# Five full expert tiles taken out of the first choice and computed around the boundary between attention and the experts

## The chip, the cores and the metric

The kernel runs on one core of one Trainium2 chip. The metric is the device time of one execution in microseconds (us); lower is better. The engines are named as in the profile: PE (TensorE), DVE (VectorE), ACT (ScalarE), POOL (GpSimd) and SP (SyncE, which here only issues DMAs). The fp32 operands of the large products are taken as pairs of fp16 numbers, a high part and what is left of it ("hi" and "lo" in many names).

## The reference

```python
def reference(x, ctx_1024, g_xattn, g_ffn, ...):      # x: (4, 2048, 512), context: (4, 77, 512)
    x = x + tanh(g_xattn) * xattn(layernorm(x), ctx_1024)   # layer norm, q, 16 heads of 64, softmax, w_out, gate
    # mixture of experts: 8 true experts and 2 null ones, top 2 of 10
    weights, selected = top_k(softmax(x @ gate_w.T + gate_b), 2)
    true_weights = weights * (selected < 8)
    norm_w = true_weights / (sum(true_weights) or 1)
    out = sum over the chosen true experts e of norm_w * (LN(x) @ expert_w[e] + expert_b[e])
    return x + tanh(g_ffn) * out
```

The text of the last lines is shortened: the experts get layernorm(x) of the new x. There are 8192 tokens, so that every token has two choices, each for a true expert or for none.

## The kernel before, in words

The program has three blocks, and all engines meet at the end of each.

**fold_context** (118 us) turns the context and the attention weights into two small matrices for each batch.

**attend** (L591) goes over the 8192 tokens in 64 tiles of 128. It is a software pipeline: each engine has a function `step` for a turn i (it calls the parts for tile i, i-1, i-2, ...) and a function `tail` for the last turns, i = 64 to 67. The order of the calls in `step` and `tail` is the order on the engine. In turn i, PE multiplies the scores of tile i (L908) and the mix of tile i-2 (L923); DVE does the softmax of tile i-1 (L1133, L1135), the new x of tile i-3 (`residual`, L1152) and its statistics, and after POOL's power (`y_rstd`, L1499) the normalized y (`y_normalize`, L1169); ACT and POOL split y in two fp16 parts (L1042, L1503); SP transposes them by DMA (`turn_y`, L809) and stores x and y to `comb` in HBM (`store`, L828); PE multiplies the gate logits (`gate`, L955, one turn later). The last tile's y is transposed by PE (L939, "turn_last") and its gate comes last. Four tiles are a group. For each group DVE finds the two experts of every token and its place among the tokens of that expert (L1195 to L1330), with running counts in `placed`, and POOL writes the entries (token number, weight, mean, 1/std) into `table` with eight indirect DMAs a group (`scatter`, L1597). The table has a region of 64 tiles for each of 8 experts and each of 2 choices.

At the end PE sums the counts of all 16 groups (`totals`, L1002), DVE rounds them up to tiles (`count_tiles`, L1609 to L1621) and works out which expert and which place in the table each tile of the list has (`find_tiles(0)`, L1627 to L1635). ACT multiplies the experts' bias (L1090), which SP loads with the last DMA of the block (L889).

**run_experts** (L1667) goes over tiles of 128 tokens of one expert, first all tiles of choice 0, then those of choice 1, in passes of five (`RING`); the number of tiles is rounded up to full passes, which gives 50 tiles in choice 0 and 70 in choice 1. For a tile, SP loads its slice of the table (`slots`, L1769, at a place read into a register, L1775), DVE makes the token numbers (L1940), POOL gathers x of 128 tokens (L1799), ACT normalizes it (L1908), PE transposes it (L1862, 4 instructions), ACT and DVE split it (L1900, L1953), PE multiplies (L1875, 12 instructions), DVE adds the bias and x (L1963, L1988), and POOL scatters the result (L1820): back to `comb` in choice 0, to the output in choice 1. PE begins the block with 14 matmuls of no use (`WARM`, L1854) while the first slots and tokens come. POOL has the last scatters of the table between the gathers of tiles 3 and 4, and DVE runs `find_tiles(1)` while it waits for the first tile.

## Time and profile before

| | |
|---|---|
| median of 3 runs | 1365.33 us (1365.13 to 1366.55) |
| the profiled execution | 1363.62 us, span 1361.8 us |
| fold_context | 0 to 118.9 us |
| attend | 118.9 to 959.4 us, PE busy 821 of 840 |
| run_experts | 959.4 to 1361.8 us, PE busy 378 of 402 |
| PE, DVE, ACT, POOL busy | 96%, 81%, 55%, 50% of the span |
| granted TensorE clock, mean | 0.982 |

The span is the time on the engines; the execution's own time is 1.8 us longer. Times in a row count from the span's start. A row of the timeline gives the start, the duration, the engine, the line and what it did; in brackets stands the idle time before it and what released it. "Issue" is time in which the engine waited for nothing that the profile shows.

### The profile page before, as it was taken

To read this page: it belongs to the slowest core of one execution; us is meant where nothing else is said; L and a number is where in the kernel's file an instruction comes from. 1 tells how busy PE (TensorE), PEld (TensorE's weight loads), DVE (VectorE), ACT (ScalarE), POOL (GpSimd) and SP (SyncE) were. 2 spreads that over 40 slices of the span, in tenths; PEclk is the share of its full clock that TensorE was granted. 3 is DMA by queue.
4 is the path that set the end of the run, shared out by engine and by line. 5 is a ranking of instruction groups with operands and counts; after the bars stand their busy time and mean duration, and the time that the engine had idled before them with its cause. 6 is when DMAs were issued, how large, how long until landed. Compare 5 with 4: busy or idle time off the path is not lost. (4 is left out here: it accounts for less than half of the span.)

```text
span 1361.8 us, 30170 instructions
## 1 busy us (share of the span) xinstructions
PE 1302.1 (96%) x7339; PEld 674.7 (50%) x7340; DVE 1109.2 (81%) x2797; ACT 752.8 (55%) x2724; POOL 686.4 (50%) x645
## 2 busy tenths in 40 slices
PE   7999999999999999999999999996699988999997
PEld 5434555555555555555555555553355544555554
DVE  5776888998998998998998999987577765777775
ACT  4755666656656656656656656663444433444442
POOL 1501233446445455455455455445676755776674
PEclk9999999999999999999999999998799998999999
DMA  8144888778978778978778978877355535787773
GB/s 310 54 170 129 184 195 193 182 186 200 243 183 192 181 181 210 239 180 193 180 180 212 238 180 194 181 160 194 80 163 163 160 130 178 234 250 244 242 240 117
DMA packets 413298, 256.17 MB, mean 188 GB/s; under 512 B 338979, under 2 KB 350307, under 8 KB 413077
## 3 DMA queue, kind: packets, MB, share of 16 engines
q1 hardware_dynamic: 385365, 180.89, 54.9%
q0 software_dynamic: 27840, 74.18, 17.3%
q8 instruction: 41, 0.67, 0.2%
q14 instruction: 52, 0.43, 0.1%
HBM read 111.61 MB, written 75.01 MB: 137 GB/s over the span
## 5 line engine op out<-in xcount | busy, mean ns | idle before, releaser
L1023 ACT ACTIVATE expd<-scores,less 128x77 f32<-128x77 f32 x1024 | 317.4, 328 | 183.0 <-DVE less L1127 182.0
L908 PE MATMUL scores<-arena,zT 128*128 (+2 forms) x2304 | 414.8, 339 | 3.4 <-PEq L159 3.4
L923 PE MATMUL mix<-u_sb,pT 128*128 128x512 f16 x1728 | 383.5, 380 | 1.3 <-DMA pT<-p_parts 0.7
L1875 PE MATMUL out_bank<-arena,expert_yT 128*128 x1440 | 336.1, 384 | 0.0
L908 PEld LDWEIGHTS scores<-arena,zT 128*128 128x128 f16 x2304 | 220.7, 98 | 170.0 <-issue 5.8
L923 PEld LDWEIGHTS mix<-u_sb,pT 128*128 128x128 f16 x1728 | 168.8, 98 | 198.5 <-DVE x_out L1152 1.4
L1875 PEld LDWEIGHTS out_bank<-arena,expert_yT 128*128 128x128 f16 x1440 | 142.5, 99 | 148.1 <-issue 7.5
L1023 ACT ACTIVATION_READ_ACCUMULATOR expd<-scores,less 128x1 f32 x1024 | 213.5, 209 | 0.0
L1597 POOL DMA_INDIRECT table<-payload,row_i x128 | 159.7, 1248 | 60.1 <-issue 34.9
L1900 ACT CAST expert_yT<-yT_bank 128x512 f16<-128x512 f32 x120 | 70.2, 585 | 182.6 <-PE yT_bank L1862 180.9
L1494 POOL TENSOR_TENSOR z_parts<-z,z_parts 128x512 f16<-128x512 f32 x62 | 71.7, 1156 | 193.4 <-ACT z_parts L1014 193.4
L1988 DVE SCALAR_TENSOR_TENSOR result<-out_bank,slots,biased 128x512 f32<-128x512 f32 x120 | 90.1, 751 | 70.5 <-PE out_bank L1875 68.1
L1499 POOL TENSOR_TENSOR x_moments<-x_spread,minus_half 128x1 f32<-128x1 f32 x64 | 65.0, 1015 | 131.3 <-DVE x_spread L1162 131.2
L1953 DVE TENSOR_TENSOR expert_yT<-yT_bank,expert_yT 128x512 f16<-128x512 f32 x120 | 83.0, 691 | 46.6 <-ACT expert_yT L1900 45.0
L1125 DVE TENSOR_REDUCE top<-scores 128x5 f32<-128x385 f32 (+1 forms) x192 | 111.4, 580 | 3.5 <-PE scores L908 3.4
L1135 DVE SCALAR_TENSOR_TENSOR expd<-expd,inverse 128x1232 f32<-128x1232 f32 x64 | 92.3, 1442 | 2.2
L1799 POOL DMA_INDIRECT two_ring<-comb,token x66 | 71.1, 1077 | 45.1 <-issue 31.6
L1143 DVE TENSOR_TENSOR p_parts<-expd,p_parts 128x1232 f16<-128x1232 f32 x64 | 91.8, 1435 | 0.2 <-issue 0.2
L1862 PE MATMUL yT_bank<-ident,expert_y 128*128 128x128 f32 x480 | 74.7, 279 | 17.2 <-ACT expert_y L1908 13.7
L1820 POOL DMA_INDIRECT out_dram<-result,token_out x70 | 72.9, 1042 | 28.2 <-issue 19.0
L1862 PEld LDWEIGHTS yT_bank<-ident,expert_y 128*128 128x128 f32 x480 | 59.7, 143 | 44.2 <-ACT expert_y L1908 20.6
L1035 ACT CAST p_parts<-expd 128x1232 f16<-128x1232 f32 x64 | 77.7, 1214 | 0.0
(183 smaller groups left out, 1643.2 us busy)
## 6 DMA issues: line engine op xcount, KB each, us to landing
comb<-x_out SPq DMA_DIRECT2D x64, 512.0 KB, 3.2
x_ln<-in_x_dram SPq DMA_DIRECT2D x64, 256.0 KB
x_res<-in_x_dram SPq DMA_DIRECT2D x64, 256.0 KB, 2.8
w_raw<-in_L_ffn_expert_w_dram SPq DMA_DIRECT2D x64, 128.0 KB, 2.3
u_dram<-u_stage SPq DMA_DIRECT2D x12, 512.0 KB, 2.8
u_sb<-u_dram SPq DMA_DIRECT2D x6, 1024.0 KB, 7.6
arena<-in_L_xattn_w_kv_dram SPq DMA_DIRECT2D x4, 1024.0 KB, 7.5
slots<-table SPq DMA_DIRECT2D x150, 2.0 KB
```

The lines of the kernel that those rows point to most:

```text
L908: last = pe.matmul(scores[s][k][:, 0:n], zT[:, s, zp, t, :], m, start=(t == 0 and (zp, mp) == PRODUCTS[0]), stop=(t == DT - 1 and (zp, mp) ...
L923: last = pe.matmul(mix[:], pT[:, s, pp, k, :], u_sb[:, k, up, :], start=(k == 0 and (pp, up) == PRODUCTS[0]), stop=False)
L1023: last = act.activation(expd[:, s, h * KEYS:(h + 1) * KEYS], scores[s][k][:, at:at + KEYS], ACT.Exp, bias=less[:, s, h:h + 1], scale=1.0 / ...
L1035: act.copy(p_parts[:, 0, 0:COLS], expd[:, s, :]).then_inc(p_hi_ready, 1)
L1125: dve.tensor_reduce(top[:, s, h0:h0 + nh], bank, AX_X, ALU.max).then_inc(top_ready, 1)
L1135: dve.scalar_tensor_tensor(e, e, P_SCALE, inverse[:, s].unsqueeze(2).broadcast_to([P, HEADS, KEYS]), ALU.mult, ALU.mult).then_inc(p_ready, 1)
L1143: dve.tensor_tensor(p_parts[:, 1, 0:COLS], expd[:, s, :], p_parts[:, 0, 0:COLS], ALU.subtract).then_inc(p_lo_ready, 1)
L1597: pool.indirect_dma_start(table, bass.IndirectOffsetOnAxis(ap=self.row_i[:, side, TOP_K * t + k:TOP_K * t + k + 1], axis=0), self.payload[ ...
L1862: last = pe.transpose(c.yT_bank[s][:, t, :], y[:, s, t * P:(t + 1) * P], ident[:])
L1875: last = pe.matmul(c.out_bank[s][:], yT[:, s, yp, t, :], w_of[:, bass.ds(e, 1), t, wp * D:(wp + 1) * D].rearrange("p a n -> p (a n)"), sta ...
L1953: dve.tensor_tensor(yT[:, s, 1], c.yT_bank[s][:], yT[:, s, 0], ALU.subtract).then_inc(c.y_lo_ready, 1)
L1988: dve.scalar_tensor_tensor(result[:, s, :], c.out_bank[buffer(s)][:], own, biased[:, buffer(s), :], ALU.mult, ALU.add).then_inc(c.result_r ...
```

## The change

Five tiles of choice 0 are taken out of the experts' passes. They are tiles that are full after twelve of the sixteen groups; the counts of twelve groups are enough to know five of them.

- PE sums the counts at the end of turn 60, and waits in turn 61, ahead of `gate`, until DVE has read them. DVE finds experts and places of the five tiles in 17 small instructions spread over turn 61 (`head_1` to `head_13`), and what is taken from each expert in 5 more in turn 62 (`take_1` to `take_4`). At the end of turn 62 it waits for the five table slices and makes the token numbers.
- SP loads the five slices in turn 62 (`fetch_head`: a register load and five DMAs behind the second transposition of p).
- POOL gathers three of the tiles at the end of turn 63 and two in the tail of turn 64, ahead of four scatters of the table. `result` is cleared at the start of attend.
- ACT normalizes them and casts the high parts (`split_head`, tails of turns 64 and 65), POOL subtracts the low parts (`low_head`, tails of 65 and 66), SP transposes them (`turn_head`), two ahead of the last `turn_y` and three behind it.
- PE multiplies three of them after `totals`, in attend's block, and two at the start of the experts' block, in place of the 14 matmuls of no use.
- DVE finishes them at the start of the experts' block (`finish_head`, two instructions a tile): two ahead of the first tokens, three behind. POOL scatters one ahead of the first gathers, four between the fourth gather and the last scatters of the table. `find_tiles(1)` moves into the first pass, in two parts, behind tiles 0 and 1. The transposes of tile 1 wait until all five are finished.
- Choice 0 has five tiles fewer in its list: 45 in place of 50. The `PSUM` banks are shared between the blocks, buffers are laid out in another order, and the semaphores of the first block are freed and used again.

```diff
+HEAD_GROUP = GROUPS - 4
+HEAD_BANKS = (3, 1, 2, 4, 5)
+HEAD_SOON = 3
...
+            def fetch_head():
+                sp.wait_ge(listing.head_listed, 1)
+                spots = table.rearrange("(p t) w -> p t w", p=P)
+                places = nc.values_load_multi_w_load_instructions(
+                    listing.head_at[0:1, :], (sp.engine,), min_val=0, max_val=TABLE_TILES - 1,
+                    skip_runtime_bounds_check_because="head_13 clamps it")[1]
+                for j, place in enumerate(places):
+                    sp.dma_start(listing.head_slots[:, j, :],
+                                 spots[:, bass.ds(place, 1), :].rearrange("p a w -> p (a w)")).then_inc(
+                                     listing.head_entry_in, 16)
...
+            def turn_head(j):
+                sp.wait_ge(listing.head_lo_ready, j + 1)
+                sp.dma_start_transpose(out=head_yT[:, j].rearrange("p l t q -> p (l t) q"),
+                                       in_=head_parts(ln, j).rearrange("p l d -> p (l d)")).then_inc(listing.head_yT_in[j], 16)
...
+                if isinstance(i, int) and i == TILES - 2:
+                    fetch_head()
...
+                if i == TILES + 1:
+                    turn_head(0)
+                    turn_head(1)
+                if i == TILES + 2:
+                    turn_head(2)
+                    turn_head(3)
+                    turn_head(4)
...
+                    if isinstance(i, int) and i == TILES - 3:
+                        pe.wait_ge(listing.head_done, 1)
...
+                if isinstance(i, int) and i == TILES - 4:
+                    pe.wait_ge(listing.head_placed_ready, GROUPS - 3)
+                    pe.matmul(totals, ones16[:], listing.head_placed[:], start=True, stop=True).then_inc(
+                        listing.head_counted, 1)
...
+            pe.wait_ge(w_lo_ready, TILES)
+            multiply_head(nc, pe, listing, banks, head_yT, w_parts, range(HEAD_SOON))
...
+            def split_head(j):
+                act.wait_ge(listing.head_got[j], 16)
+                act.activation(head_y[j], listing.result[:, j, :], ACT.Identity, bias=listing.head_slots[:, j, 2:3],
+                               scale=listing.head_slots[:, j, 3:4]).then_inc(listing.head_y_ready, 1)
+                act.wait_ge(listing.head_y_ready, j + 1)
+                act.copy(head_parts(ln, j)[:, 0], head_y[j]).then_inc(listing.head_hi_ready, 1)
...
+                    act.wait_ge(z_lo_ready, TILES)
+                    act.wait_ge(zT_in[0], landed(TILES - 2, 0))
+                    split_head(0)
+                    split_head(1)
+                if i == TILES + 1:
+                    split_head(2)
+                    split_head(3)
+                    split_head(4)
...
+                heads = isinstance(i, int) and i == TILES - 3
+                takes = isinstance(i, int) and i == TILES - 2
...
+                if heads:
+                    listing.head_1(dve, totals)
+                if takes:
+                    listing.take_1(dve)
...
+                    listing.head_13(dve)
+                if takes:
+                    dve.wait_ge(listing.head_entry_in, 16 * RING)
+                    own = listing.head_slots[:, :, 0:1]
+                    dve.tensor_scalar(listing.head_token[:], own, 2.0, None, ALU.mult).then_inc(listing.head_token_ready, 1)
...
+            listing.find_owners(dve, 0)
+            listing.find_places(dve, 0).then_inc(listing.listed, 1)
...
+            def gather_head(j):
+                pool.wait_ge(listing.head_token_ready, 1)
+                pool.wait_ge(listing.result_clear, 1)
+                halves = comb[0:HEAD_GROUP * GROUP * P].rearrange("n (l d) -> (n l) d", l=2)
+                pool.indirect_dma_start(listing.result[:, j, :], None, halves,
+                                        bass.IndirectOffsetOnAxis(ap=listing.head_token[:, j, :], axis=0),
+                                        bounds_check=halves.shape[0] - 1, oob_is_err=False).then_inc(listing.head_got[j], 16)
+            def low_head(j):
+                pool.wait_ge(listing.head_hi_ready, j + 1)
+                parts = head_parts(ln, j)
+                pool.tensor_tensor(parts[:, 1], head_y[j], parts[:, 0], ALU.subtract).then_inc(listing.head_lo_ready, 1)
...
             def tail(i, s, turn):
                 ps, t = 1 - s, (i - 3) % GROUP
                 if live(i - 3):
                     y_rstd(i - 3, ps, t)
                 if i == TILES:
+                    gather_head(3)
+                    gather_head(4)
+                if i == TILES + 2:
+                    low_head(2)
+                    low_head(3)
+                    low_head(4)
+                if i == TILES:
                     scatter(GROUPS - 3, ((1, 1), (2, 0), (2, 1), (3, 0)))
                 if i == TILES + 1:
                     scatter(GROUPS - 3, ((3, 1),))
                     scatter(GROUPS - 2, ((0, 0),), by_choice=True)
+                    low_head(0)
+                    low_head(1)
...
+                if isinstance(i, int) and i == TILES - 1:
+                    gather_head(0)
+                    gather_head(1)
+                    gather_head(2)
...
+            pool.memset(listing.result[:].rearrange("p s d -> p (s d)"), 0.0).then_inc(listing.result_clear, 1)
             run(pool, step, tail)
...
+def multiply_head(nc, pe, listing, banks, head_yT, w_parts, tiles):
+    w_of = w_parts.rearrange("p (e t) x -> p e t x", t=DT)
+    pe.wait_ge(listing.head_listed, 1)
+    chosen = nc.values_load_multi_w_load_instructions(
+        listing.head_expert[0:1, tiles.start:tiles.stop], (pe.engine,), min_val=0, max_val=EXPERTS - 1,
+        skip_runtime_bounds_check_because="head_9 clamps it")[1]
+    for j, e in zip(tiles, chosen):
+        pe.wait_ge(listing.head_yT_in[j], 16)
+        for t in range(DT):
+            for yp, wp in PRODUCTS:
+                last = pe.matmul(banks[HEAD_BANKS[j]][:], head_yT[:, j, yp, t, :],
+                                 w_of[:, bass.ds(e, 1), t, wp * D:(wp + 1) * D].rearrange("p a n -> p (a n)"),
+                                 start=(t == 0 and (yp, wp) == PRODUCTS[0]),
+                                 stop=(t == DT - 1 and (yp, wp) == PRODUCTS[-1]))
+        last.then_inc(listing.head_summed, 1)
...
+        dve.wait_ge(self.taken_ready, 4)
+        self.after(dve, dve.tensor_tensor(self.tiles_f[:], self.tiles_i[:], self.taken[:], ALU.subtract))
+        dve.tensor_tensor(self.held[:], self.tiles_f[:], self.taken_turn[:], ALU.subtract)
...
+            def scatter_head(j):
+                pool.wait_ge(listing.head_result, j + 1)
+                pool.wait_ge(listing.head_token_ready, 2)
+                pool.indirect_dma_start(halves, bass.IndirectOffsetOnAxis(ap=listing.head_token_out[:, j, :], axis=0),
+                                        result[:, j, :], None, bounds_check=halves.shape[0] - 1,
+                                        oob_is_err=False).then_inc(listing.head_put[j], 16)
...
+            scatter_head(0)
             for j in range(LEAD):
                 gathers(choices[0], j, j)
+            for j in range(1, R):
+                scatter_head(j)
...
-            for n in range(WARM):
-                again = pe.matmul(spare_bank[:], w_of[:, 0, n % DT, 0:P], w_of[:, 1, n % DT, 0:D], start=True, stop=True)
-            again.then_inc(warmed, 1)
+            multiply_head(nc, pe, listing, banks, head_yT, w_parts, range(HEAD_SOON, R))
...
+                elif c.k == 0 and j == 1:
+                    pe.wait_ge(listing.head_result, R)
...
+            head_experts = nc.values_load_multi_w_load_instructions(
+                listing.head_expert[0:1, :], (dve.engine,), min_val=0, max_val=EXPERTS - 1,
+                skip_runtime_bounds_check_because="head_9 clamps it")[1]
+            def finish_head(j):
+                own = listing.head_slots[:, j, 1:2]
+                dve.scalar_tensor_tensor(result[:, j, :],
+                                         expert_bias[:, bass.ds(head_experts[j], 1), :].rearrange("p a n -> p (a n)"), own,
+                                         result[:, j, :], ALU.mult, ALU.add).then_inc(listing.head_biased, 1)
+                dve.wait_ge(listing.head_biased, j + 1)
+                dve.wait_ge(listing.head_summed, j + 1)
+                dve.scalar_tensor_tensor(result[:, j, :], banks[HEAD_BANKS[j]][:], own, result[:, j, :], ALU.mult,
+                                         ALU.add).then_inc(listing.head_result, 1)
...
+            finish_head(0)
+            finish_head(1)
             for j in range(R):
                 if j in (0, FIRST):
                     dve.wait_ge(entry_in[j // FIRST], 16 * (FIRST if j == 0 else R - FIRST))
                 name_token(choices[0], 0, j, j)
-            listing.find_tiles(dve, 1).then_inc(listing.listed, 1)
+            for j in range(2, R):
+                finish_head(j)
...
+                    if c.k == 0 and first_pass(r) and s == 0:
+                        listing.find_owners(dve, 1)
+                    if c.k == 0 and first_pass(r) and s == 1:
+                        listing.find_places(dve, 1).then_inc(listing.listed, 1)
```

POOL at the end of attend, before: from `y_low(60)` on (L1597 is `scatter`, L1499 `y_rstd`, L1503 `y_low`).

```order
L1503 TENSOR_TENSOR y_parts<-y,y_parts 128x512
L1597 DMA table<-payload,row_i 135168x4 x3
L1499 TENSOR_TENSOR x_moments<-x_spread,minus_half 128x1
L1597 DMA table<-payload,row_i 135168x4 x4
L1499 TENSOR_TENSOR x_moments<-x_spread,minus_half 128x1
L1597 DMA table<-payload,row_i 135168x4 x2
L1499 TENSOR_TENSOR x_moments<-x_spread,minus_half 128x1
L1597 DMA table<-payload,row_i 135168x4 x9
```

The same stretch of the change, behind `y_low(60)` (L1864 is `scatter`, L1601 `y_rstd`, L1621 `gather_head`, L1628 `low_head`).

```order
L1864 DMA table<-payload,row_i 135168x4 x3
L1621 DMA result<-comb,head_token 128x512 x3
L1601 TENSOR_TENSOR x_moments<-x_spread,minus_half 128x1
L1621 DMA result<-comb,head_token 128x512 x2
L1864 DMA table<-payload,row_i 135168x4 x4
L1601 TENSOR_TENSOR x_moments<-x_spread,minus_half 128x1
L1864 DMA table<-payload,row_i 135168x4 x2
L1628 TENSOR_TENSOR z_parts<-z,z_parts 128x512
L1628 TENSOR_TENSOR arena<-z,arena 128x512
L1601 TENSOR_TENSOR x_moments<-x_spread,minus_half 128x1
L1628 TENSOR_TENSOR arena<-x_ln,arena 128x512 x2
L1628 TENSOR_TENSOR arena<-gamma,arena 128x512
L1864 DMA table<-payload,row_i 135168x4 x9
```

The five gathers stand ahead of `y_rstd` of tiles 61 and 62, and two of the subtractions ahead of that of tile 63.

SP at the end of attend, before, from the last transpositions of p on (L824 `turn_p_lo`, L809 `turn_y`, L828 `store`, L889 the experts' bias).

```order
L824 DMA_TRANSPOSE pT<-p_parts 128x10x128
L809 DMA_TRANSPOSE yT<-y_parts 128x8x128
L778 DMA x_res<-in_x_dram 128x512
L828 DMA comb<-x_out 256x1x512
L809 DMA_TRANSPOSE yT<-y_parts 128x8x128
L828 DMA comb<-x_out 256x1x512
L889 DMA u_sb<-in_L_ffn_expert_b_dram 128x4096
```

The same stretch of the change (L831, L816, L835, L922; L852 is `turn_head`, L785 the load of x).

```order
L831 DMA_TRANSPOSE pT<-p_parts 128x10x128
L816 DMA_TRANSPOSE yT<-y_parts 128x8x128
L785 DMA x_res<-in_x_dram 128x512
L835 DMA comb<-x_out 256x1x512
L852 DMA_TRANSPOSE arena<-z_parts 128x8x128
L852 DMA_TRANSPOSE arena<-arena 128x8x128
L816 DMA_TRANSPOSE yT<-y_parts 128x8x128
L835 DMA comb<-x_out 256x1x512
L852 DMA_TRANSPOSE arena<-arena 128x8x128 x3
L922 DMA u_sb<-in_L_ffn_expert_b_dram 128x4096
```

Two transpositions of the five tiles stand ahead of the last `turn_y`, which is that of tile 62, and three ahead of the load of the bias.

POOL at the start of the experts, of the change (L2097 is `scatter_head`, L2069 the gathers, L1864 the scatters of the table; before, the block began with one scatter of the table, four gathers and five scatters of the table).

```order
L1864 DMA table<-payload,row_i 135168x4
L2097 DMA comb<-result,head_token_out 16384x512
L2069 DMA one_ring<-comb,token 128x512 x4
L2097 DMA comb<-result,head_token_out 16384x512 x4
L1864 DMA table<-payload,row_i 135168x4 x5
```

One scatter of a result has gone ahead of the first gather, and four ahead of the five scatters of the table and the fifth gather.


## Rows read from the trace of the kernel before

**Rows 1.** Timeline of PE, end of attend and start of the experts.

```profile
939.43 0.18 PE L955 MATMUL routing<-gate_parts,yT 128*128 128x20 f16 x1 [0.45 <-DMA yT<-y_parts]
...
942.01 1.12 PE L939 MATMUL scores<-ident,y 128*128 128x128 f32 x4 [2.23 <-DVE y L1169]
...
950.43 0.19 PE L1002 MATMUL routing<-placed,ones 128*128 128x16 f16 x1 [1.91 <-DVE placed L1313]
959.50 4.53 PE L1854 MATMUL spare_bank<-arena 128*128 128x512 f16 x14 [8.88 <-PEq L598]
```

**Rows 2.** Busy time by stretch: length, each engine, PEclk, DMA share, GB/s.

```profile
942.00:962.00 20.00, 4.54 (x24) 2.26 (x25) 11.49 (x66) 6.75 (x4) 10.72 (x10) 0.50 0.31 110
...
970.00:975.00 5.00, 4.81 (x14) 2.28 (x15) 2.00 (x4) 2.38 (x4) 3.78 (x5) 0.50 0.19 52
```

**Rows 3.** Chain that ended last, start of the experts: start, us, what.

```profile
959.46 0.75 SPq L1775
...
961.00 1.67 DMA slots<-table
...
963.76 3.43 DMA one_ring<-comb,token
...
971.31 4.92 PE out_bank L1875 x12
976.23 0.44 PE yT_bank L1862 x4
976.66 2.59 PE out_bank L1875 x12
```

**Rows 4.** Timeline of DVE, turn 62 and the last turns of attend.

```profile
911.58 0.25 DVE L1133 RECIPROCAL inverse<-total 128x16 f32<-128x16 f32 x1 [1.41 <-ACT expd L1023]
...
928.17 0.54 DVE L1169 TENSOR_SCALAR y<-x_out,x_moments 128x512 f32<-128x512 f32 x1
...
931.42 0.69 DVE L1152 SCALAR_TENSOR_TENSOR x_out<-mix,x_res 128x512 f32<-128x512 f32 x1 [0.24 <-PE mix L928]
...
934.13 0.55 DVE L1169 TENSOR_SCALAR y<-x_out,x_moments 128x512 f32<-128x512 f32 x1 [0.47 <-POOL x_moments L1499]
...
938.83 0.69 DVE L1152 SCALAR_TENSOR_TENSOR x_out<-mix,x_res 128x512 f32<-128x512 f32 x1 [0.93 <-PE mix L928]
...
941.41 0.55 DVE L1169 TENSOR_SCALAR y<-x_out,x_moments 128x512 f32<-128x512 f32 x1 [0.69 <-POOL x_moments L1499]
```

**Rows 5.** Timeline of SP (its queue), same stretch and the slots.

```profile
906.90 1.53 SPq L824 DMA_TRANSPOSE pT<-p_parts  x1
...
936.27 1.27 SPq L809 DMA_TRANSPOSE yT<-y_parts  x1
...
960.47 6.12 SPq L1769 DMA_DIRECT2D slots<-table  x10
```

**Rows 6.** Timeline of POOL, same stretch.

```profile
920.58 1.16 POOL L1503 TENSOR_TENSOR y_parts<-y,y_parts 128x512 f16<-128x512 f32 x1 [4.81 <-ACT y_parts L1042]
...
933.40 0.69 POOL L1499 TENSOR_TENSOR x_moments<-x_spread,minus_half 128x1 f32<-128x1 f32 x1
...
938.83 0.98 POOL L1597 DMA_INDIRECT table<-payload,row_i  x1 [3.24 <-DVE payload L1330]
...
944.72 1.05 POOL L1597 DMA_INDIRECT table<-payload,row_i  x1 [3.34 <-issue]
```

**Rows 7.** Timeline of POOL, the fifth gather of the experts.

```profile
975.92 1.04 POOL L1799 DMA_INDIRECT one_ring<-comb,token  x1 [0.30 <-issue]
```

**Rows 8.** Timeline of ACT, end of attend.

```profile
948.55 3.62 ACT L1090 ACTIVATE u_sb<-u_sb 128x4096 f32<-128x4096 f32 x1 [1.42 <-DMA u_sb<-in_L_ffn_expert_b_dram]
```

**Rows 9.** Timeline of DVE, one y in turn 61.

```profile
895.91 1.50 DVE L1169 TENSOR_SCALAR y<-x_out,x_moments 128x512 f32<-128x512 f32 x1
```

**Rows 10.** Chain that ended last, after 45 tiles of the experts.

```profile
1109.40 3.41 issue
...
1113.89 3.64 PE out_bank L1875 x12
```

More of the change, by code:

```diff
@@ new lines, in __init__ @@
+        self.head_got = [sem(f"head_got{s}") for s in range(RING)]
+        self.head_y_ready = sem("head_y_ready")
+        self.head_hi_ready = sem("head_hi_ready")
+        self.head_lo_ready = sem("head_lo_ready")
+        self.head_yT_in = [sem(f"head_yT_in{s}") for s in range(RING)]
+        self.head_summed = sem("head_summed")
+        self.head_biased = sem("head_biased")
+        self.head_result = sem("head_result")
+        self.head_put = [sem(f"head_put{s}") for s in range(RING)]
```

185 lines of the change are left out of this document (159 added, 26 removed).

## The prediction

> **What bounds the kernel now.** I read the page's slices first: PE is busy nine tenths or more of almost every slice. The timeline of PE then shows where it isn't: at the end of attend [rows 1]. From 939.43 to 959.50 PE does under 5 us of work. It waits for DVE's last y (2.23 us idle before 942.01), sums the counts at 950.43 and is idle for 8.88 us until the next block's matmuls of no use. So this stretch is bound by latency: one chain over DVE, POOL, SP and PE, in which each microsecond put into any link is paid in full. The windows show the clock with it [rows 2]: granted 0.50 (1.2 GHz) from 942 to 962 and again from 970 to 975, where the mean of the span is 0.98 of 2.4 GHz. The chain of waits through the start of the experts [rows 3] is a register load (0.75), slots (1.67 to land), a gather (3.43), then tile 0, which multiplies for 4.92 us at the low clock. Later tiles take 2.59 and 0.44 for their transposes, and follow one another: 3.03 each.
>
> **What is saved.** One pass of choice 0 is five tiles: 5 x 3.03 = 15.1 us [rows 3]. That holds only as far as the rest isn't lengthened. The multiplication of the five tiles is not saved but moved to where PE is idle; what the change must win is the idle time at the boundary.
>
> **What is added, link by link.** DVE's 17 small instructions in turn 61 and 5 in turn 62 (about 0.1 us each, an estimate) I cost at nothing: DVE was idle for 1.41 us at the end of a turn, waiting for ACT [rows 4]. If the cover is short, up to 17 x 0.1 is added, in the range.
>
> 1. *The five table slices.* SP issues them behind `turn_p_lo(61)`, which ends at 906.90 + 1.53 = 908.4 [rows 5]. A register load (0.75), five issues at 6.12/10 = 0.61 and 1.67 to land [rows 3, 5] give 913.9. DVE waits for them at the end of turn 62, where it went on at 911.58 [rows 4]. With the token numbers: 914.2, **+2.6**. Everything behind on DVE goes with it, the y that POOL waits for too.
> 2. *Three gathers ahead of `y_rstd(61)`.* POOL's subtraction ended at 920.58 + 1.16 = 921.7 [rows 6]; with 2.6 it is 924.3. Three scatters at 0.98 + 0.30 [rows 6, 7] give 928.3 with their lag, three gathers at 1.04 + 0.30 [rows 7] 932.4, the power (0.6) 933.1: y(61) begins there instead of at 928.17 [rows 4], +5.0. Of that the 0.24 us idle before x_out(62) is taken up: +4.8 there.
> 3. *Two gathers ahead of `y_rstd(62)`.* From 933.1: two gathers 2.7, four scatters 5.1, the power 0.6 [rows 6, 7]: y(62) at 941.7 instead of 934.13 [rows 4], +7.6. In the trace DVE then worked until 938.83 - 0.93, so 3.8 us: x_out(63) at 945.6 instead of 938.83.
> 4. *Two subtractions ahead of `y_rstd(63)`.* The scatter at 938.83 began 0.93 us after DVE's payload [rows 4, 6], so now at 946.5, and takes 0.98. Two subtractions of 1.16 end at 950.0. y(63) follows at about 950.7 instead of 941.41.
> 5. *SP.* `turn_head(1)` waits for the second subtraction and stands ahead of `turn_y(62)`. A transposition holds the queue 1.3 us, so that of y(62) is issued at 951.6. In the trace its gate came 939.43 - 936.27 = 3.2 us behind the issue [rows 1, 5]: 954.8. The transposes of y(63) stand behind that gate on PE: 955.0 instead of 942.01, **+13.0**. This contains links 1 to 4. SP's order costs 3.7 of it, since y(63) alone would have let PE begin at 951.3.
> 6. *From there to the counts* nothing moves: 8.42 us [rows 1], totals at 963.4. The three last `turn_head` and the bias load end on SP at 959; the bias needs 8.4 us to land by the page, and ACT 3.6 for its multiplication [rows 8], which ends at about 971, beside link 7.
> 7. *PE's three tiles.* A register load 0.75 and 36 matmuls. At 2.59/12 they take 7.8; a start at the low clock cost the 14 of `WARM` 4.53 - 3.02 = 1.5 more and tile 0 2.3 more [rows 1, 3]. I take 9.5 in all. So PE ends at 963.6 + 10.3 = 973.9, where DVE and POOL needed 8.88 us behind the counts [rows 1]: PE is last by 1.4. The block's change is about 0.2 to 0.3. The experts begin at 974.1 instead of 959.50: **+14.6**.
> 8. *The start of the experts.* DVE loads five registers and runs four instructions of some 0.8 ahead of the first tokens: 4.0 to 4.2 us against 3.2 until the slots came, **+1.0**. POOL has four scatters of a result (4 x 1.3) ahead of the fifth gather. That gather was issued at 975.92 [rows 7] and lands 3.4 later; PE needed its y at about 982.3, with 0.8 for ACT: a slack of some 2.1 against 5.2 later: **+3.1** before tile 3 or 4. Two tiles in place of `WARM` (24 against 14 matmuls) end while PE waits anyhow.
>
> The Trainium skill, page "DMA: Bandwidth & Descriptors", section "Anatomy of one DMA — SWDGE (gpsimd) path", gives a DMA about 2.0 us and its bytes over 436e3. That would be an estimate of 2.6 us for the 256 KB of a gather; the row has 3.43 [rows 3], and I use the row. By the page the stall before tile 4 would be 0.8 shorter.
>
> Another row speaks against the change. One y took 1.50 us in turn 61 instead of 0.54, as a POOL subtraction ran beside it [rows 4, 9]. The change puts five such subtractions into the tail, where DVE is on the chain; I count none of them as hit, and up to 1 us for each of two in the range. The Trainium skill, page "SBUF — State Buffer", section "SBUF: two separate sides", says why: DVE and GpSimd share one pair of ports, which whoever starts first has until its instruction ends. By that rule alone the sum would be about 1 to 2 us higher.
>
> **The sum.** 14.6 + 1.0 + 3.1 - 15.1 = **+3.6 us**. Against the profiled execution that is 1363.6 + 3.6 = 1367.2. The median of the runs shown lies 1.7 above it, so I forecast 1368.9. A difference of 0.2% (2.7 us) is about what a measurement of this kernel can tell from none: "the same" is 1362.6 to 1368.1.
>
> **Rivals.**
>
> *A, SP's order costs nothing (chance 0.20).* The slices land before DVE asks for them, and y(62) isn't held by the transpositions ahead of it. For: SP had over 2 us between its DMAs there, and the landing may overlap the issues more than I have it. Against: the order on SP is fixed. It decides where y(63) and not gate(62) releases the transposes. It gives back 2.6 and 3.7: 1368.9 - 6.3 = 1362.6, the edge of faster and the same.
>
> *B, the stall behind the 45th tile goes (0.18).* PE was idle there for 3.41 us for no reason that the profile shows, and multiplied the next tile in 3.64 instead of 2.59 [rows 3, 10]; with 0.6 for its transposes at the low clock these are 5.1 us on the way to choice 1. It came at the end of a loop. A program of another layout may not have it: 1363.8.
>
> *C, POOL pauses on the chain (0.13).* Behind the last `y_rstd` POOL did nothing for 3.34 us, for no reason shown, with work in its queue [rows 6]. Then it cost nothing. If it stands ahead of a subtraction or `y_rstd` now, each of the links behind is later by it: 1368.9 + 3.3 = 1372.2.
>
> *D, the list isn't shorter (0.03).* If the counts still fill ten passes, nothing is saved: 1384.
>
> **Numbers.** The forecast has 0.46: 0.04 faster, 0.12 the same (its terms for the start and the clock may be 1 us too high), 0.30 slower. A: 0.14 faster, 0.06 the same. B: 0.07, 0.10, 0.01 slower. C and D are slower. Together 0.25, 0.28 and 0.47. The range goes from 1361.0 (A, with 1.5 less from the start) to 1374.0 (C, with two blocked DVE instructions); it leaves out D and the ends of A and C, where the low end would be A and B together, 1357.5.
>
> **What would show it.** DVE idle 2.6 us before the inverse of turn 63; y(61), y(62) and y(63) later by about 5, 8 and 9 us; the transposes of the last y released by SP's DMA and not by DVE; PE the last engine of attend with 36 matmuls; the experts' block at 974; a PE idle of about 3 us before tile 3 or 4 with POOL's gather as its releaser; 115 tiles of transposes in place of 120. I am wrong if the block begins before 971, if no stall stands before tile 4, or if PE's tiles after the start are slower than 3.03.

## The result and the profile after

The changed kernel is slower: 1371.43 us median (1369.81 to 1374.14, 7 runs), where the kernel before took 1365.63 us (1363.82 to 1368.93, 7 runs). The ratio is 1.0038, with a 95% interval of 1.0026 to 1.0050, so 5.2 us more (3.6 to 6.8). The forecast was 3.6 us more.

The page of the changed kernel:

```profile
span 1369.9 us, 30121 instructions
...
PE 1305.6 (95%) x7306; PEld 672.4 (49%) x7307; DVE 1107.8 (81%) x2821; ACT 753.8 (55%) x2724; POOL 697.9 (51%) x651
...
PEclk9899999999999999999999999997799999999999
```

The rows of a trace are of one execution. The profiled execution took 1371.68 us, 8.1 more than that of before (1363.62). Some of this is not the change's. The block `fold_context` ended 2.5 us later in this execution: DVE's first instruction of attend is at 121.46 and not at 119.00. Over the profiled executions of all versions of the two kernels in this study it lies between 118.32 and 121.53, and the latest is one whose first block is that of the kernel before. So the stages are compared from that instruction on. Stage "attend" goes from it to the first issue of `slots` in the experts' block, stage "experts" from there to the end of the span.

| | attend | experts | both |
|---|---|---|---|
| before | 841.5 | 401.3 | 1242.8 |
| changed | 857.7 | 390.8 | 1248.4 |
| difference | +16.2 | -10.6 | +5.6 |
| forecast | +14.6 | -11.0 | +3.6 |

The timeline of DVE around the boundary, which answers to [rows 4]:

```profile
917.36 0.17 DVE L1507 TENSOR_SCALAR head_token<-head_slots 128x5 int32<-128x5 f32 x1 [4.02 <-DMA head_slots<-table]
...
917.51 0.25 DVE L1190 RECIPROCAL inverse<-total 128x16 f32<-128x16 f32 x1
...
937.24 0.60 DVE L1226 TENSOR_SCALAR y<-x_out,x_moments 128x512 f32<-128x512 f32 x1 [3.56 <-POOL x_moments L1601]
...
945.78 0.60 DVE L1226 TENSOR_SCALAR y<-x_out,x_moments 128x512 f32<-128x512 f32 x1 [3.28 <-POOL x_moments L1601]
...
951.74 0.69 DVE L1209 SCALAR_TENSOR_TENSOR x_out<-bank,x_res 128x512 f32<-128x512 f32 x1 [2.14 <-PE bank L961]
...
954.35 1.37 DVE L1226 TENSOR_SCALAR y<-x_out,x_moments 128x512 f32<-128x512 f32 x1 [0.72 <-POOL x_moments L1601]
```

The first row is the wait for the table slices (4.02 us; at the same place DVE had been idle for 1.41 us before the change). Further, y(61) and y(62) wait 3.56 and 3.28 us for POOL, where y(61) had not waited and y(62) 0.47. x_out(63) has a wait for PE that the forecast didn't have, 2.14 us. The last y takes 1.37 us and not 0.55.

The timeline of POOL [rows 6], with the gathers ahead of the powers (L1601) and the subtractions of the five tiles (L1628):

```profile
926.50 1.16 POOL L1605 TENSOR_TENSOR y_parts<-y,y_parts 128x512 f16<-128x512 f32 x1 [4.81 <-ACT y_parts L1083]
...
932.15 1.83 POOL L1621 DMA_INDIRECT result<-comb,head_token  x1 [0.30 <-issue]
...
936.62 0.59 POOL L1601 TENSOR_TENSOR x_moments<-x_spread,minus_half 128x1 f32<-128x1 f32 x1
...
950.53 0.99 POOL L1864 DMA_INDIRECT table<-payload,row_i  x1 [3.58 <-DVE payload L1389]
951.52 1.19 POOL L1628 TENSOR_TENSOR z_parts<-z,z_parts 128x512 f16<-128x512 f32 x1
...
953.74 0.58 POOL L1601 TENSOR_TENSOR x_moments<-x_spread,minus_half 128x1 f32<-128x1 f32 x1
954.28 2.45 POOL L1628 TENSOR_TENSOR arena<-x_ln,arena 128x512 f16<-128x512 f32 x2
```

The timeline of SP [rows 5] and of PE [rows 1]:

```profile
909.92 1.43 SPq L831 DMA_TRANSPOSE pT<-p_parts  x1
913.47 2.54 SPq L846 DMA_DIRECT2D head_slots<-table  x5
...
955.57 1.23 SPq L816 DMA_TRANSPOSE yT<-y_parts  x1
```

```profile
930.38 7.69 PE L956 MATMUL bank<-u_sb,pT 128*128 128x512 f16 x27 [3.31 <-DVE x_out L1209]
...
942.93 8.35 PE L956 MATMUL bank<-u_sb,pT 128*128 128x512 f16 x27 [2.84 <-DMA pT<-p_parts]
...
959.06 1.10 PE L972 MATMUL bank<-ident,y 128*128 128x128 f32 x4
...
968.59 9.42 PE L1706 MATMUL bank<-arena 128*128 x36 [1.03 <-issue]
...
1006.07 1.11 PE L2145 MATMUL bank<-ident,expert_y 128*128 128x128 f32 x4 [3.67 <-ACT expert_y L2191]
```

PE is idle ahead of each of its two last mixes (3.31 and 2.84 us) and after them. It is the gate of tile 62, behind SP's transposition of 955.57, that lets the transposes of the last y begin (959.06). The head tiles take 9.42 us. In the experts' block the transposes of tile 4 come after 3.67 us of idle time, and the clock falls again (0.60 in the last row below). The clock by stretch, which answers to [rows 2] (length, busy time of PE, PEld, DVE, ACT, POOL, granted clock, DMA share, GB/s):

```profile
940.00:953.00 13.00, 9.05 (x41) 3.67 (x37) 6.96 (x32) 6.40 (x10) 8.25 (x9) 0.74 0.58 152
...
991.00:996.00 5.00, 5.00 (x16) 1.96 (x15) 1.41 (x3) 2.24 (x3) 3.78 (x5) 0.55 0.53 204
1006.00:1010.00 4.00, 3.93 (x13) 2.03 (x14) 1.41 (x3) 3.20 (x5) 3.35 (x3) 0.60 0.67 197
```

### The profile page after: what moved, and what is told of

The parts are those of the page before. It is cut to its first block and busy times, and to the rows that moved or that the text cites. A ratio compares the mean times of both kernels' runs of the same rounds, so it can differ in the third digit from the quotient of the medians.

```text
span 1369.9 us, 30121 instructions
## 1 busy us (share of the span) xinstructions
PE 1305.6 (95%) x7306; PEld 672.4 (49%) x7307; DVE 1107.8 (81%) x2821; ACT 753.8 (55%) x2724; POOL 697.9 (51%) x651
## 5 line engine op out<-in xcount | busy, mean ns | idle before, releaser
L941 PE MATMUL bank<-arena,zT 128*128 (+2 forms) x2304 | 414.9, 338 | 3.4 <-PEq L164 3.4
L1064 ACT ACTIVATE expd<-bank,less 128x77 f32<-128x77 f32 x1024 | 317.3, 328 | 182.8 <-DVE less L1184 181.6
L956 PE MATMUL bank<-u_sb,pT 128*128 128x512 f16 x1728 | 387.5, 382 | 6.2 <-DVE x_out L1209 3.3
L2158 PE MATMUL bank<-arena,expert_yT 128*128 x1380 | 323.3, 385 | 0.0
L941 PEld LDWEIGHTS bank<-arena,zT 128*128 128x128 f16 x2304 | 220.7, 98 | 170.0 <-issue 5.7
L956 PEld LDWEIGHTS bank<-u_sb,pT 128*128 128x128 f16 x1728 | 169.9, 98 | 206.4 <-issue 8.3
L1064 ACT ACTIVATION_READ_ACCUMULATOR expd<-bank,less 128x1 f32 x1024 | 213.5, 208 | 0.0
L2158 PEld LDWEIGHTS bank<-arena,expert_yT 128*128 128x128 f16 x1380 | 136.9, 99 | 143.3 <-issue 9.5
L1864 POOL DMA_INDIRECT table<-payload,row_i x128 | 159.3, 1245 | 63.8 <-issue 31.6
L2273 DVE SCALAR_TENSOR_TENSOR result<-bank,slots,biased 128x512 f32<-128x512 f32 x115 | 86.3, 751 | 67.0 <-PE bank L2158 64.6
L1601 POOL TENSOR_TENSOR x_moments<-x_spread,minus_half 128x1 f32<-128x1 f32 x64 | 64.1, 1002 | 132.2 <-DVE x_spread L1219 132.1
L2236 DVE TENSOR_TENSOR expert_yT<-bank,expert_yT 128x512 f16<-128x512 f32 x115 | 79.5, 691 | 46.3 <-ACT expert_yT L2183 40.9
L1182 DVE TENSOR_REDUCE top<-bank 128x5 f32<-128x385 f32 (+1 forms) x192 | 111.3, 579 | 4.1 <-PE bank L941 3.4
L2069 POOL DMA_INDIRECT two_ring<-comb,token x66 | 74.9, 1135 | 40.5 <-issue 20.2
```

The lines of the kernel that those rows point to most:

```text
L941: last = pe.matmul(scores[s][k][:, 0:n], zT[:, s, zp, t, :], m, start=(t == 0 and (zp, mp) == PRODUCTS[0]), stop=(t == DT - 1 and (zp, mp) ...
L956: last = pe.matmul(mix[:], pT[:, s, pp, k, :], u_sb[:, k, up, :], start=(k == 0 and (pp, up) == PRODUCTS[0]), stop=False)
L1064: last = act.activation(expd[:, s, h * KEYS:(h + 1) * KEYS], scores[s][k][:, at:at + KEYS], ACT.Exp, bias=less[:, s, h:h + 1], scale=1.0 / ...
L1182: dve.tensor_reduce(top[:, s, h0:h0 + nh], bank, AX_X, ALU.max).then_inc(top_ready, 1)
L1864: pool.indirect_dma_start(table, bass.IndirectOffsetOnAxis(ap=self.row_i[:, side, TOP_K * t + k:TOP_K * t + k + 1], axis=0), self.payload[ ...
L2158: last = pe.matmul(c.out_bank[s][:], yT[:, s, yp, t, :], w_of[:, bass.ds(e, 1), t, wp * D:(wp + 1) * D].rearrange("p a n -> p (a n)"), sta ...
```

## The experiments

Each is the changed kernel with the edit shown, unless it says otherwise. The ratio is to the kernel before; "attend" and "experts" are the stages defined above, in the profiled execution.

| | median us | ratio (95%) | profiled us | attend | experts |
|---|---|---|---|---|---|
| before | 1365.63 | 1 | 1363.62 | 841.5 | 401.3 |
| changed | 1371.43 | 1.0038 (1.0026 to 1.0050) | 1371.68 | 857.7 | 390.8 |
| e1 | 1368.57 | 1.0028 (1.0017 to 1.0038) | 1368.49 | 857.3 | 388.5 |
| e2 | 1368.05 | 1.0029 (1.0016 to 1.0042) | 1369.59 | 856.2 | 392.5 |
| e3 | 1366.69 | 1.0017 (1.0007 to 1.0027) | 1364.64 | 857.5 | 387.1 |
| e4 | 1369.89 | 1.0040 (1.0026 to 1.0055) | 1370.17 | 857.5 | 392.1 |
| e5 | 1368.29 | 1.0021 (1.0007 to 1.0034) | 1364.01 | 854.6 | 388.0 |
| e6 | 1363.04 | 0.9981 (0.9970 to 0.9992) | 1361.08 | 850.1 | 390.2 |
| e7 | 1358.55 | 0.9953 (0.9936 to 0.9969) | 1356.09 | 847.2 | 386.9 |
| e8 | 1347.86 | 0.9863 (0.9837 to 0.9888) | 1351.24 | 840.7 | 387.2 |

Executions of the kernel before, run beside these, had medians of 1364.68 (e1 to e4) and 1365.25 (e5 to e8), from 1360.1 to 1370.2. A difference between two experiments of less than some 2 us is not resolved by the ratios; where less matters, there are only the rows, of one execution each. How well those repeat can be read from the table: attend took 857.7 and 857.5 us in the changed kernel and in e3, whose edit is in the experts' block. The experts' block is the same in the changed kernel, e1, e2, e4, e5 and e6, and took 388.0 to 392.5. So a difference of 4 us in the last column alone shows nothing.

### e1: the transposition of y(62) ahead of those of the head tiles

```diff
-                if i == TILES + 1:
-                    turn_head(0)
-                    turn_head(1)
                 if i == TILES + 2:
+                    turn_head(0)
+                    turn_head(1)
                     turn_head(2)
```

> The changed kernel with one edit: on SP, the two transpositions of head tiles that stood ahead of that of y(62) stand behind it, with the other three. Theory 1 (the order on SP holds the gate of tile 62, which stands ahead of the transposes of the last y on PE): these transposes come at y(63) + 0.6 us instead of 4.7 us behind it, so that the boundary is 3.5 to 4 us earlier and the kernel at about the time before plus 1.5 us. Rival (the transposition of y(62) is slow for the traffic of the gathers and not for its place in the queue, or PE's three head tiles then wait for their own transpositions): less than 1.5 us gained.

The timelines of DVE, of POOL and of PE:

```profile
953.97 3.58 DVE L1225 TENSOR_SCALAR y<-x_out,x_moments 128x512 f32<-128x512 f32 x1 [0.84 <-POOL x_moments L1600]
```

```profile
953.90 2.25 POOL L1627 TENSOR_TENSOR arena<-x_ln,arena 128x512 f16<-128x512 f32 x2
956.12 1.14 POOL L1627 TENSOR_TENSOR arena<-gamma,arena 128x512 f16<-128x512 f32 x1
```

```profile
957.60 1.12 PE L971 MATMUL bank<-ident,y 128*128 128x128 f32 x4 [6.02 <-DVE y L1225]
```

Counted from the start of attend, the transposes of the last y come at 836.7 instead of 837.6, only 0.9 us earlier. Now DVE's last y releases them (6.02 us of idle time, "<-DVE y"), and this y takes 3.58 us. Meanwhile POOL does its subtractions of the tiles 2 to 4 of the five (953.90 to 957.26). SP's order was what the wait named, but another wait nearly as long stood under it. The rival's amount came (less than 1.5 us), but for neither of its reasons: by these rows the order counts for 0.9 us.

### e2: the tokens a turn later

```diff
-                if takes:
+                if isinstance(i, int) and i == TILES - 1:
                     dve.wait_ge(listing.head_entry_in, 16 * RING)
```

> The changed kernel with one edit: DVE waits for the five table slices at the end of turn 63 and not of turn 62. Theory 1: the wait of 4.0 us is gone, as the slices have long landed, and POOL's gathers, which stand at the end of turn 63, are not later for it, so that everything from turn 63 on comes 3 us earlier and the kernel is 2.5 to 3 us faster than the changed one. Rival (PE or the gathers bound these turns, and DVE catches up): under 1 us, with y(61) no earlier than in the changed kernel.

```profile
932.16 0.60 DVE L1226 TENSOR_SCALAR y<-x_out,x_moments 128x512 f32<-128x512 f32 x1 [3.56 <-POOL x_moments L1601]
...
949.26 3.58 DVE L1226 TENSOR_SCALAR y<-x_out,x_moments 128x512 f32<-128x512 f32 x1 [1.12 <-POOL x_moments L1601]
```

```profile
953.95 1.09 PE L972 MATMUL bank<-ident,y 128*128 128x128 f32 x4
...
963.45 10.71 PE L1706 MATMUL bank<-arena 128*128 x36 [1.03 <-issue]
```

The wait is gone, and y(61) begins at 813.1 us of attend instead of 815.8. The transposes come 2.7 us earlier too, as theory 1 has it. But the 36 matmuls then take 10.71 us and not 9.42, at a granted clock of 0.74 against 0.84. Attend is 1.5 us shorter, not 2.7. The ratios (1.0038 and 1.0029, 1.2 us) don't separate the two kernels; theory 1's 2.5 to 3 us in the time did not come.

### e3: the fifth gather first

```diff
-            for j in range(LEAD):
+            for j in range(R):
                 gathers(choices[0], j, j)
...
-                    if live(LEAD) and not (c.k == 0 and first_pass(r) and s + LEAD < LEAD):
+                    if live(LEAD) and not (c.k == 0 and first_pass(r) and s + LEAD < R):
```

> The changed kernel with one edit: at the start of the experts the fifth gather stands ahead of the four scatters of results, not behind them and the five scatters of the table. Theory 1: PE's idle time of 3.67 us before the transposes of tile 4 goes, and the fall of the clock with it, 5.3 us together. Rival (the scatters come later now and DVE's first results wait for them, since they reuse the same buffers): half of it comes back as a wait of DVE for a landed scatter, 2.5 us gained.

```profile
1000.69 2.76 PE L2158 MATMUL bank<-arena,expert_yT 128*128 x12 [1.48 <-ACT expert_yT L2183]
...
1007.16 0.66 PE L2145 MATMUL bank<-ident,expert_y 128*128 128x128 f32 x4 [0.68 <-ACT expert_y L2191]
```

```profile
997.33 0.77 DVE L1902 TENSOR_TENSOR past<-past,held 128x600 f16<-128x600 f16 x1
...
999.61 0.20 DVE L1908 TENSOR_SCALAR tile_at<-ahead 128x75 int32<-128x75 f32 x1
...
999.80 0.69 DVE L2236 TENSOR_TENSOR expert_yT<-bank,expert_yT 128x512 f16<-128x512 f32 x1
```

The idle time of 3.67 us before tile 4 is gone; waits of 1.48 and 0.68 us stand in its place. The first is put down to ACT, but ACT's cast for that tile had ended at 996.60. DVE was late: it had the second part of `find_tiles(1)` (L1902 to L1908) ahead of its own half of the split (L2236), which ended at 1000.49, 0.2 us before the multiplication. That is work which the change moved into the first pass, and in the changed kernel the stall before tile 4 hid it; e7 shows the same wait (1.49 us). Neither wait is, as the rival had it, one for a landed scatter.

From the first issue of `slots` to the last pass of choice 0 e3 takes 140.4 us, where the versions with the changed kernel's order took 141.9 to 143.5 (the changed kernel 143.4). The ratios differ by 2.9 us (1.0038 to 1.0017), give or take 2.1. So 5.3 us of theory 1 is too much, and the rival's 2.5 fits in amount and not in its reason.

### e4: gathers of 8 KB

```diff
-                pool.indirect_dma_start(listing.result[:, j, :], None, halves,
+                pool.indirect_dma_start(listing.result[:, j, 0:16], None, halves.rearrange("n (c x) -> (n c) x", x=16),
```

> The changed kernel with gathers of the five head tiles that bring 16 columns of some early rows instead of 512 of the right ones (8 KB instead of 256 KB each), so the five tiles' results are not those of the reference. POOL's order and its count of instructions stay. Theory 1 (POOL's time for issuing decides): y(61) to y(63) as in the changed kernel, within 0.5 us. Rival (the traffic of the gathers delays the DMA of p(63) and with it mix(63), which began 2.0 us behind x_out(62)): mix(63) begins right behind x_out(62), runs at the full clock, and the boundary comes 2 to 4 us earlier.

```profile
938.37 7.48 PE L956 MATMUL bank<-u_sb,pT 128*128 128x512 f16 x27 [0.91 <-DVE x_out L1209]
...
956.39 1.09 PE L972 MATMUL bank<-ident,y 128*128 128x128 f32 x4
```

```profile
946.88 0.69 DVE L1209 SCALAR_TENSOR_TENSOR x_out<-bank,x_res 128x512 f32<-128x512 f32 x1
...
951.72 3.58 DVE L1226 TENSOR_SCALAR y<-x_out,x_moments 128x512 f32<-128x512 f32 x1 [2.96 <-POOL x_moments L1601]
```

Mix(63) begins right behind x_out(62) (0.91 us idle, "<-DVE x_out", where it had been 2.84 "<-DMA pT"). Counted from the start of attend, mix(63) begins at 819.5 us, against 821.5 to 822.9 in the changed kernel, e1 and e3, which have the gathers of 256 KB. So the rival is right in that these gathers delayed the DMA of p(63) by some 2 us; they landed 6.4 us after their issue (median of the five), and those of 8 KB 2.8. Mix(63) did not run at the full clock, as the rival had it: it took 7.48 us at a granted 0.80. x_out(63) comes 2.2 us earlier, counted from the start of attend. And it buys nothing: y(63) waits 2.96 us for POOL, whose subtractions stand ahead of the power, and then takes 3.58 us. The transposes come at 837.5 us, as in the changed kernel (837.6), and attend is as long within 0.2 us. They stand behind both POOL's subtractions, on which SP's transpositions of the head tiles wait, and y(63), which waits for POOL as well. So POOL's queue decides; the traffic hides under it.

### e5: the five subtractions on DVE

With e1's edit, and with the load of the bias ahead of the last two `turn_head`; on DVE two of the subtractions stand ahead of x_out(63), one ahead of y(63), two behind it (the cut leaves out where they are called):

```diff
-                    low_head(0)
-                    low_head(1)
...
+            def low_head(j):
+                dve.wait_ge(listing.head_hi_ready, j + 1)
+                parts = head_parts(ln, j)
+                dve.tensor_tensor(parts[:, 1], head_y[j], parts[:, 0], ALU.subtract).then_inc(listing.head_lo_ready, 1)
```

> The changed kernel with the SP order of e1, and the five subtractions of low parts taken from POOL to DVE, into its waits of the last two turns; the load of the bias goes ahead of the last two transpositions. In e1 y(63) took 3.58 us, while POOL's subtractions ran, instead of 0.55 us, and so took the place of SP's queue as what PE waits for. Theory 1 (POOL's subtractions hold DVE, by place and by port): y(63) takes 0.55 us and begins 1 to 2 us earlier, the transposes of the last y come 4 us earlier than in e1, and the time falls by 3 to 4 us against e1. Rival (the subtractions cost as much on DVE, 0.69 each, since DVE's chain is the longest there): 1 us or less against e1.

```profile
947.75 0.69 DVE L1513 TENSOR_TENSOR z_parts<-z,z_parts 128x512 f16<-128x512 f32 x1
...
949.63 0.69 DVE L1208 SCALAR_TENSOR_TENSOR x_out<-bank,x_res 128x512 f32<-128x512 f32 x1 [0.59 <-PE bank L960]
...
952.58 0.55 DVE L1225 TENSOR_SCALAR y<-x_out,x_moments 128x512 f32<-128x512 f32 x1 [0.46 <-POOL x_moments L1612]
```

```profile
940.30 8.85 PE L955 MATMUL bank<-u_sb,pT 128*128 128x512 f16 x27 [1.97 <-DMA pT<-p_parts]
...
953.18 1.12 PE L971 MATMUL bank<-ident,y 128*128 128x128 f32 x4 [3.20 <-DVE y L1225]
...
963.92 9.25 PE L1706 MATMUL bank<-arena 128*128 x36 [2.04 <-issue]
```

y(63) takes 0.55 us again, the subtractions 0.69 each, and the transposes begin 3.2 us earlier than in e1 (833.5 us of attend against 836.7). Nearly all of it is the shorter y(63), which begins only 0.2 us earlier and not 1 to 2, as theory 1 had it. Attend is 2.7 us shorter than e1's. The rows of the stage are for theory 1, and the time of the whole leaves it open: the ratios, 1.0028 and 1.0021, don't separate the two. The profiled execution, 1364.01 us, is the fastest of the twelve of this version (up to 1371.53, median 1368.29), so its rows say little of what the slower ones lose; no trace of those is kept. What the rows do show as lost again is 2.04 us of "issue" ahead of the head tiles (1.19 in e1), and a mix(63) of 8.85 us at a granted 0.67 (8.27 in e1).

### e6: the gathers behind the powers

```diff
-                if isinstance(i, int) and i == TILES - 1:
-                    gather_head(0)
-                    gather_head(1)
-                    gather_head(2)
...
                 if i == TILES:
-                    gather_head(3)
-                    gather_head(4)
-                    scatter(GROUPS - 3, ((1, 1), (2, 0), (2, 1), (3, 0)))
+                    gather_head(0)
+                    gather_head(1)
+                    gather_head(2)
+                    scatter(GROUPS - 3, ((1, 1),))
                 if i == TILES + 1:
-                    scatter(GROUPS - 3, ((3, 1),))
-                    scatter(GROUPS - 2, ((0, 0),), by_choice=True)
+                    gather_head(3)
+                    gather_head(4)
+                    scatter(GROUPS - 3, ((2, 0), (2, 1)))
                 if i == TILES + 2:
-                    scatter(GROUPS - 2, ((1, 0), (2, 0), (3, 0), (0, 1), (1, 1)), by_choice=True)
+                    scatter(GROUPS - 3, ((3, 0), (3, 1)))
+                    scatter(GROUPS - 2, ((0, 0), (1, 0), (2, 0), (3, 0), (0, 1), (1, 1)), by_choice=True)
```

> e5 with one more edit: POOL's gathers stand behind the powers for y(61) and y(62) and not ahead of them, and five scatters of the table wait behind them in their place. Theory 1 (POOL's queue ahead of the powers was the cost): y(61) and y(62) lose their waits of 3.6 and 3.3 us for POOL, x_out(62) and x_out(63) come 4 to 6 us earlier, and the time falls by 4 to 6 us against e5. Rival (the traffic of the gathers holds the DMA of p(63), so mix(63) and all behind it stay): less than 2 us.

```profile
931.24 0.54 DVE L1225 TENSOR_SCALAR y<-x_out,x_moments 128x512 f32<-128x512 f32 x1
...
938.89 0.55 DVE L1225 TENSOR_SCALAR y<-x_out,x_moments 128x512 f32<-128x512 f32 x1 [0.47 <-POOL x_moments L1612]
...
946.71 0.55 DVE L1225 TENSOR_SCALAR y<-x_out,x_moments 128x512 f32<-128x512 f32 x1 [0.47 <-POOL x_moments L1612]
```

y(61) and y(62) wait no longer than before the change. Attend is 4.5 us shorter than e5's, and the time goes from 1.0021 to 0.9981 of before, 5.5 us: theory 1, within its range. The kernel is now 2.6 us faster than the one before (1.1 to 4.1).

### e7: all of it

e6 with the edits of e2 and e3.

> e6 with the edits of e2 (tokens a turn later) and e3 (fifth gather first). Theory 1 (the costs lie one behind the other and add): the block of the experts begins 3 to 5 us later than before the change and not 16, and the kernel takes 1356 to 1360 us, 6 to 8 us less than before the change. Rival (taking waits away uncovers others behind them, as in e1): 1361 to 1364 us.

```profile
926.45 6.00 PE L955 MATMUL bank<-u_sb,pT 128*128 128x512 f16 x27 [0.60 <-DVE x_out L1208]
...
935.20 5.99 PE L955 MATMUL bank<-u_sb,pT 128*128 128x512 f16 x27 [1.99 <-DMA pT<-p_parts]
...
945.85 0.66 PE L971 MATMUL bank<-ident,y 128*128 128x128 f32 x4 [1.67 <-DVE y L1225]
...
956.58 9.85 PE L1703 MATMUL bank<-arena 128*128 x36 [2.46 <-issue]
```

The time is 1358.55 us, 0.9953 of the kernel before (0.9936 to 0.9969), 6.4 us less. That is the time that theory 1 has. The boundary is later than it has it: attend is 5.8 us longer than before the change, not 3 to 5, of the 16.2 that it was. Both mixes run at the full clock now (6.00 and 5.99 us, granted 1.00). The transposes of the last y take 0.66 us.

### e8: the kernel before, one pass less

```diff
+        self.after(dve, dve.tensor_scalar(self.passes[:, 0:1], self.passes[:, 0:1], -1.0, None, ALU.add))
         self.after(dve, dve.tensor_scalar(self.inner_passes[:], self.passes[:], 2.0, -2.0, ALU.max, ALU.add))
```

> The kernel before, told to do one pass of choice 0 less (one more small instruction on DVE), so that the last five tiles of choice 0 are not computed at all. It measures what the five tiles are worth in the passes. Theory 1: 15.1 us less than before. Rival (some of a pass is hidden by what choice 1 waits for, or the idle time at the loop's end changes): 12 us or less.

```profile
1100.13 0.63 PE L1863 MATMUL yT_bank<-ident,expert_y 128*128 128x128 f32 x4 [2.71 <-issue]
```

PE begins the last pass of choice 0, after 2.71 us of idle time, 978.6 us after the start of attend; in the kernel before it was 993.8. That is 15.2 us, of which 0.7 is less idle time at the loop's end. The two stages together take 14.9 us less than before in the profiled executions (1227.9 against 1242.8), and the ratio says 18.7 us with an interval of 15.3 to 22.3. So one pass is worth 14.9 us by the rows and at least 15.3 by the ratio, about the 15.1 that the forecast took, or more; the rival (12 or less) is out. The two don't contradict each other: the profiled execution, 1351.24 us, is the slowest of the four of e8 (the fastest took 1345.09), and that of before is 2 us below its median. What the faster executions of e8 do otherwise is open; no trace of them is kept.

## Why the prediction was right, and where it was off

**The direction and the mechanism are right.** The time saved in the passes is smaller than what a chain bound by latency lost. The transposes waited for SP's DMA, PE was the last engine of attend, the experts' block began late, and PE stood before tile 4, all as forecast. The loss stands at the links named: y(61), y(62), y(63) are later by 6.6, 9.2 and 10.5 us counted from the start of attend (forecast 5.0, 7.6, 9.3), the transposes by 14.6 (13.0), the experts' block by 16.2 (14.6).

**The saving** ("5 x 3.03 = 15.1 us"): right by the rows of e8 (14.9); by the ratio it may be too small, 15.3 to 22.3.

**Link 1, the slices: mis-sized.** The forecast had 0.75 us for SP's register load. Between the end of `turn_p_lo(61)` (911.35) and the first issue (913.47) lie 2.1 us; the five issues then take 2.54 and not 3.05. DVE waited 4.02 us, where it had waited 1.41 for ACT, and from one inverse to the next the turn was 3.0 us longer; another 0.5 had come up before it, so the inverse is 3.5 later and not 2.6. e2 shows that the wait is worth 2.7 us of the chain.

**Link 2: 0.7 us more.** The sum took a POOL request at about 1.3; among the six, one scatter took 1.43 and one gather 1.83. With the 0.9 of link 1 this is the error of 1.6 us that y(61) and y(62), the transposes and the end of the stage all show.

**Links 3 and 4: one hidden under the other.** x_out(63) is 10.5 us later and not 6.8. Mix(63) waited for the DMA of p(63), which was late by the traffic of the gathers (e4), and took 8.35 us at a granted clock of 0.71, against 5.99 at 1.00 before the change. The forecast had neither. It cost nothing, since POOL's two subtractions held y(63) anyway (e4 again).

**Link 5, SP's order: wrong in what it is worth.** The forecast had 3.7 us for it, "since y(63) alone would have let PE begin at 951.3". e1 took it away and gave back 0.9. The step missed that y(63) itself takes 3.58 us while POOL subtracts. The text had that cost in its range ("up to 1 us for each of two") and none in the sum; at this one instruction it is 3.0. The Trainium skill, page "SBUF — State Buffer", section "SBUF: two separate sides", says that of a GpSimd instruction and a VectorE one in a 2-port perf mode (or with two SBUF inputs), whichever starts first keeps the shared ports for its whole instruction. e1's rows agree with such a block, and they go further: y(63) ended only when three POOL subtractions in a row had ended (957.26 and 957.55), so it didn't get its turn between them either. No run here shows in which mode this instruction runs; that the ports are the cause is argued, and that the neighbourhood of the subtractions is, e5 shows. With the subtractions on DVE (e5) it takes 0.55. In the changed kernel it took 1.37, under the cover of SP's order.

**Link 7: right**, within what repeats. 36 matmuls in 9.42 (forecast 9.5), and PE is the last engine of attend. In the other versions the same 36 took 9.25 to 10.71.

**Link 8: the place right, the price too low.** Tile 0 is 1.5 us later after the first slots (9.14 against 7.68; forecast 1.0). The stall before tile 4 cost 3.67 of idle time, 0.6 more around its transposes (1.11 against 0.60 us, without the overlap that they have otherwise) and 1.1 for the next multiplication (3.85 against 2.75 us by the timeline) at a granted clock of 0.60 in that stretch: 5.4 against 3.1. The sum counted the wait and not the clock that goes with it. In e1, e2, e4 and e5 the same stall cost 4.7 to 6.5.

**What brought the sum near: in part luck.** The costs were 16.2 + 1.5 + 5.4 = 23.1 us against the forecast's 18.7, 4.4 too low. With the saving of 15.1 that makes +8.0, and the stages show +5.6. The rest came back where the forecast had no term: the idle time at the end of the loop was 2.70 us instead of 3.41, and from there to the end the changed kernel took 247.4 us instead of 249.0. The experiments whose code is the same there took 245.5 to 249.1, so this gain belongs to the executions profiled and not clearly to the change.

**The rivals.** A (SP's order costs nothing): its time did not come, and the slices did make DVE wait; but its half on the order is nearly true (0.9 us), for a reason that it didn't have. B: the stall at the end of the loop is there in every version, 1.90 to 3.41 us; it didn't go. C: POOL's pause of 3.34 us didn't come back on the chain; behind the last power POOL goes on with subtractions without a gap. D: the list is shorter; the page has 460 transposes in the experts in place of 480.

## What to carry to other kernels

Where a stretch is bound by one chain over several engines, work that is put into their idle time costs whatever stands ahead of the chain's next link in each queue: ask of each queue what it delays, and put the new work behind the link, not ahead of it. The edits that lead to e7 move the same work by a few places in each queue, and five subtractions to another engine, and turn 5 us of loss into 6 us of gain. A wait that a trace names may hide another of the same length: take one away and look again before you count its price, as with SP's order in e1 and with the stall before tile 4 in e3. When PE waits, look at the granted clock behind the wait as well. And the rows are of one execution: here some 2 us of the sum were made good by idle time that other versions with the same code there did not save.

## What was not expected of the hardware

- One VectorE instruction that takes 0.55 us took 3.58 us beside a row of GpSimd subtractions (e1, e2 and e4 alike), and 1.37 us in the changed kernel.
- A wait between matmuls can change what the matmuls behind it cost: mix(62) took 7.69 us after 3.31 us of idle time (granted clock 0.78) and 6.00 after 0.60 (1.00). The wait just ahead doesn't decide alone: after nearly the same one, 1.97 and 1.99 us, mix(63) took 8.85 in e5 (0.67), where mix(62) had run at 0.78, and 5.99 in e7 (1.00), where it had run at 1.00. In e2, 2.7 us won ahead of the head tiles came with 1.3 lost in them.
- The stretch with a register load on SP between two DMAs took 2.1 us, and that with the load ahead of PE's head tiles 1.03 to 2.46 ("issue"), where the load at the start of the experts had shown 0.75. What else lies in these stretches the traces don't show.
- Gathers of 256 KB delayed the DMA transposition of p by 2 us, though SP issued it and POOL the gathers (e4).
